# Last two turns of attention: first pair's rows loaded and measured sooner, normalised later, its seven splits reordered between and behind the values

## The chip, the cores and the metric

One Trainium2 chip, one core of it. The metric is the device time of one launch in microseconds. The kernel before is given by the median of three runs. Beside the times there is one profiled execution, from which all rows come.

## What is computed

The reference is one decoder layer over x, 4 sequences of 2048 tokens with 512 features, and a context of 77 tokens per sequence:

```python
x = x + ssm(layernorm(x), ...)                   # a state space layer over the first axis
x = x + xattn(layernorm(x), ctx, Wq, Wk, Wv, Wo) # 16 heads of 32, 77 keys
x = x + mlp(layernorm(x), ...)                   # 512 -> 2048 -> 512, butterflies and gelu between
```

In the kernel the butterflies are folded into two dense weight matrices first, and the MLP works with those.

## The kernel before

All products that matter are made from high and low parts: a float32 tile is copied to a rounded high part by ScalarE (`hi_...`), the low part is the difference, made by VectorE (`lo_...`), and TensorE adds three products (`split3`, L417).

**Attention turns.** The 8192 tokens are 16 groups (NG) of 512, in four tiles (T) of 128. `attn_loop` runs 18 turns, g = 0 to 17. Turn g works on three groups at once: scores and softmax of group g (`has(0)`), the preparation of queries of group g+1 (`has(1)`), values and first projections of group g-1 (`has(-1)`), last projections of group g-2 (`has(-2)`). So turn 15 (NG-1) has scores, values and projections and no queries, turn 16 (NG) has values and projections, turn 17 only projections 2 and 3. Every engine has its own list of the turn's work, written out by hand (`attn_pe`, `attn_act`, `attn_dve`, `norm` on GpSimd), and engines wait for each other by semaphores that count numbered slots. A slot is one bank of PSUM from 4 to 7 (slot number modulo 4) that TensorE fills, ScalarE copies to a high part and VectorE to a low part or adds to a row; TensorE may fill a bank again when VectorE has finished the slot before it there. Scores use banks 0 to 3. An engine never passes over an item of its list.

TensorE's list in turns 15 to 17 is: `turn_p(2,-1)` (transposes of the probabilities of tile 2), `project(2,-2)`, `scores(0)`, `turn_p(3,-1)`, `project(3,-2)`, `scores(1)`, `values(0)` to `values(3)`, `turn_p(0,0)`, `scores(2)`, `project(0,-1)`, `project(1,-1)`, `turn_p(1,0)`, `scores(3)`, less what a turn does not have. The tiles have these names in the profile: es probabilities, pth/ptl/pt the high and low parts of their transposes (p below), aoh/aol those of the values' outputs, x the rows with the attention's result added by `residual`, rmax the maximum in `shift`, rsum and rinv the sums.

**The MLP's first pair.** The MLP works on eight pairs of groups. A pair's rows are loaded to X (`load_x2`, from x2 in DRAM, where `store_x2` has put the results of attention), measured by VectorE (`spread3` for the statistics of four tiles, `moments` for the variance), given the inverse root by GpSimd (`rsqrt`), normalised in place by ScalarE (`apply3`), transposed by TensorE (`turn3`, eight times, into banks 0 to 3 for the first pair), copied to rawx by ScalarE (`raw_x`), and split into seven operands, xth and xtl: B11, T2, B21, T3, T1, T4, B22. Four of them are combinations that VectorE makes in rawx in place (`mix_x`, four of them, each of which overwrites what a split before it has read). For the first pair all this is done in turns 15 to 17, between the attention's own items; for the later pairs it is inside the MLP and is not touched.

The MLP's products for chunk c take the splits in the order B11, T2, B21, T3, T1, T4, B22 (`up`, units A11, S2, A12, S3, S1, A22, S4). The unit waits until `x_split` of its operand have been made.

**Folded weights.** One chunk of the folded weights is prepared in every turn up to 15: loaded to wc_s (`load_wc`), mixed by VectorE (`mix_weights`), rounded by ScalarE to wc_h (`high_weights`), the low part by VectorE (`low_weights`), stored (`store_wc`). SyncE issues all the DMAs, in one list. The MLP's own weights come through a ring of seven buffers, whose first loads wait for the end of `values(3)` in turn 16.

Of the kernel before, what the change touches and what calls it, by code (L numbers as in the profile page):

```python
# [20 lines left out]
def decoder_layer(nc, x, ctxT, log_dt, log_re, lam_im, vt, vinv, wqT, wkT, wvT, woT, wexpT, bexp, upbias,  # L21
# [237 lines left out]
    with ExitStack() as ctx:  # L259
# [77 lines left out]
        SPLIT_ORDER = (B11, T3, T2, B21, B22, T4, T1)  # L337
        MIX_BEFORE = {B11: 0, B21: 0, B22: 0, T3: 1, T2: 2, T4: 3, T1: 4}
# [22 lines left out]
        x_split = lambda p, o: PROD * p + SPLIT_ORDER.index(o) + 1  # L361
# [94 lines left out]
        def _(sp):  # L456
# [162 lines left out]
            load_wc(NG - 1)  # L619
            sp.wait_ge(pe_slot, SLOTS * (NG - 1))  # L620
            load_x2(0)
            load_x2(1)
            store_x2(NG - 1)
# [38 lines left out]
        def _(pool):  # L662
# [83 lines left out]
            def norm(g, has):  # L746
# [8 lines left out]
                for t in range(T):  # L755
                    pool.wait_ge(rinv_ready, T * g + t + 1)
                    e = es[t % 2][:, :, 0:CK].rearrange("p f (h k) -> p f h k", k=L)
                    r = rinv[:, t % 2, :].rearrange("p (f h) -> p f h", f=KC)
                    for f in range(KC):
                        mul = nc.gpsimd.tensor_tensor(e[:, f], e[:, f], r[:, f].unsqueeze(2).broadcast_to([P, HPC, L]), ALU.mult)  # L760
                    mul.then_inc(p_ready, 1)
                    if g == NG - 1 and t == 0:
                        rsqrt(2 * NG, xn2_ready, NG)
                    if g == NG - 1 and t == 2:
                        rsqrt(2 * NG + 1, xn3_ready, 1)
# [43 lines left out]
        def _(act):  # L809
# [114 lines left out]
            def apply3(g):  # L924
                act.wait_ge(ln_ready, 2 * NG + g + 1)
                xs = X[:, g % 2 * T:(g % 2 + 1) * T]
                apply(xs, xs, xn3_ready)
# [8 lines left out]
            def hi_x3(p, o):  # L936
                act.wait_ge(x3_raw, 8 * p + 8)
# [16 lines left out]
            def attn_act(g, has):  # L954
# [39 lines left out]
                if g == NG:  # L994
                    apply3(1)
# [3 lines left out]
                if g == NG:  # L999
                    for i in range(4, 8):  # L1000
                        raw_x(0, i, i - 4, FIRST_TURN[i])
# [3 lines left out]
                if g == NG:  # L1005
                    load_table(ACT.Gelu)
# [3 lines left out]
                    hi_x3(0, T3)  # L1010
                hi_v(0)
                hi_x(0)
                if g == NG:
                    hi_x3(0, T2)
# [3 lines left out]
                if g == NG:  # L1018
                    hi_x3(0, B21)
                hi_v(2)  # L1020
                hi_v(3)
                if 1 <= g < NG:
                    high_weights(g)
                if g == NG - 1:
                    apply3(0)
                if g == NG:
                    for o in SPLIT_ORDER[4:]:
# [5 lines left out]
                hi_p(0, 0)  # L1033
                hi_x(2)
# [77 lines left out]
        def _(dve):  # L1112
# [239 lines left out]
            def split_first(a, b):  # L1352
                for o in SPLIT_ORDER[a:b]:
                    if MIX_BEFORE[o]:
                        mix_x(0, MIX_BEFORE[o] - 1)
                    lo_x3(0, o)

# [7 lines left out]
            def attn_dve(g, has):  # L1365
# [60 lines left out]
                residual(2, -2)  # L1426
                shift(0)
                if g == NG - 1:
                    spread3(0)
                lo_p(3, -1)  # L1430
                sums(0)
                if g == NG - 1:
                    moments(2 * NG)
                residual(3, -2)
                if g == NG:
                    split_first(0, 2)
                    mix_x(0, 1)
                if g == NG + 1:
                    split_first(6, PROD)
# [5 lines left out]
                if g == NG:  # L1445
                    lo_x3(0, T2)
# [3 lines left out]
                if g == NG:  # L1450
                    split_first(3, 4)
                lo_v(2)
                lo_v(3)
                if g == NG:
                    split_first(4, 5)
# [6 lines left out]
                if g == NG - 1:  # L1462
                    spread3(1)
                lo_x(2)
                residual(0, -1)
                sums(2)
                if g == NG - 1:
                    moments(2 * NG + 1)
                lo_x(3)
                residual(1, -1)  # L1470
                if g == NG:
                    split_first(5, 6)
                lo_p(1, 0)
                shift(3)
# [3 lines left out]
                if 0 <= g < NG:  # L1478
                    low_weights(g, 0)
                sums(3)  # L1480
                if 0 <= g < NG:
# [139 lines left out]
        def _(pe):  # L1621
# [146 lines left out]
            def attn_pe(g, has):  # L1768
# [86 lines left out]
                if g == NG:  # L1855
                    for i in range(4):
                        pe.wait_ge(x3_raw, i + 1)
                        turn3(0, FIRST_TURN[4 + i], i)
# [10 lines left out]
                values(3)  # L1869
                turn_p(0, 0)  # L1870
# [163 lines left out]
```

## Time and profile before

| | us |
|---|---|
| three runs, median | 2355.14 |
| three runs, lowest and highest | 2351.54, 2356.56 |
| the profiled execution, its time | 2351.65 |
| its span | 2349.9 |
| TensorE busy in the span | 2219.8 (94%) |
| VectorE, ScalarE, GpSimd busy | 1770.7, 1291.4, 557.8 |

Times in the profile are counted from the span's start. A row of the timeline gives the start, the duration and, in brackets, how long the engine had been idle before it and what it had waited for. "x4" are four instructions in a row, given as one. The granted clock is TensorE's, as a share of full speed.

### The profile page before, as it was taken

Reading aid. Unit: us, or ns where it says so; the run is one execution under the profiler, and the core shown is the slowest. Engines: PE = TensorE matmul, PEld = TensorE weight load, DVE = VectorE, ACT = ScalarE, POOL = GpSimd, SP = SyncE. Lnnn points to the kernel's source line nnn. Section 1 sums busy time; section 2 is a strip of 40 time slices with the busy share of each in tenths; the row PEclk is TensorE's granted clock in tenths of the full one; section 3 lists DMA queues with packets and bytes.
Section 4 is the critical chain, followed back from the end, with each engine's and each line's share of the span. In section 5 each row is a group of like instructions: output and inputs, shape, how many; then the busy total and the mean of one; then the engine's idle time right before and its main releaser. Section 6 shows DMA issues by size and latency. Waiting matters only on the chain.

```text
span 2349.9 us, 42242 instructions
## 1 busy us (share of the span) xinstructions
PE 2219.8 (94%) x15752; PEld 1938.0 (82%) x15752; DVE 1770.7 (75%) x2969; ACT 1291.4 (55%) x2832; POOL 557.8 (24%) x619
## 2 busy tenths in 40 slices
PE   8777889999999999779999999999999999999998
PEld 4777668777778777658998988988989989889898
DVE  5999678888888888655866857947858768578567
ACT  2998556576576676444544635535445446355343
POOL 3788222232222222200030030120300300300203
PEclk9888879999999999999999999999999999999999
DMA  8555712332332332247667676685686686776765
GB/s 332 192 179 183 261 53 78 117 125 77 114 121 84 108 111 77 95 159 231 200 197 251 208 238 207 207 265 172 216 267 184 204 267 199 225 222 207 226 188 178
DMA packets 190883, 424.47 MB, mean 181 GB/s; under 512 B 27342, under 2 KB 64718, under 8 KB 190286
## 3 DMA queue, kind: packets, MB, share of 16 engines
q1 hardware_dynamic: 190696, 421.94, 55.6%
q8 instruction: 121, 1.98, 0.3%
q14 instruction: 66, 0.54, 0.1%
HBM read 331.29 MB, written 90.60 MB: 180 GB/s over the span
## 4 chain that ended last, share of the span: by engine, by line
PE 66%; DVE 17%; ACT 10%; issue 4%; POOL 1%; DMA 1%; DVEq 0%; ACTq 0%; SPq 0%; POOLq 0%
PE ps L417 53%; PE ps L1831 5%; ACT es L986 5%; PE ps L1799 2%; DVE st L1165 2%; DVE gl L1194 2%; DVE G L1556 2%; DVE ptl L1194 2%; PE ps L1810 1%; DVE wc_s L1194 1%; DVE rmax L1406 1%; ACT wc_h L943 1%; DVE rsum L1417 1%; ACT pth L961 1%; DVE pt L1194 1%
## 5 line engine op out<-in xcount | busy, mean ns | idle before, releaser
L417 PE MATMUL ps<-ring,gh 128*128 128x256 f32 x3584 | 654.4, 285 | 12.5 <-DVE gl L1194 12.4
L417 PEld LDWEIGHTS ps<-ring,gh 128*128 128x128 f32 x3584 | 558.0, 192 | 16.7 <-DVE gl L1194 15.7
L417 PE MATMUL ps<-xth,ring 128*128 128x512 f32 x1792 | 553.4, 389 | 1.0 <-ACT U L1082 1.0
L417 PE MATMUL ps<-ring,gl 128*128 128x256 f32 x1792 | 506.7, 283 | 0.0
L417 PEld LDWEIGHTS ps<-xth,ring 128*128 128x128 f32 x1792 | 336.4, 188 | 71.1 <-issue 1.4
L1070 ACT ACTIVATE gh<-G 128x512 fp32r<-128x512 f32 x384 | 236.8, 628 | 212.5 <-PE ps L417 212.2
L417 PE MATMUL ps<-xtl,ring 128*128 128x512 f32 x896 | 348.6, 389 | 0.0
L417 PEld LDWEIGHTS ps<-ring,gl 128*128 128x128 f32 x1792 | 343.4, 192 | 0.0
L1194 DVE TENSOR_TENSOR gl<-G,gh 128x512 fp32r<-128x512 f32 x384 | 278.1, 736 | 57.1 <-ACT gh L1070 55.5
L760 POOL TENSOR_TENSOR es<-es,rinv 128x308 f32<-128x308 f32 x256 | 180.8, 738 | 454.6 <-DVE rinv L1421 454.6
L1496 DVE TENSOR_TENSOR U<-ps,U 128x512 f32<-128x512 f32 (+1 forms) x168 | 137.2, 817 | 168.1 <-PE ps L417 165.4
L1053 ACT ACTIVATE G<-G,up_b 128x512 f32<-128x512 f32 x192 | 138.9, 723 | 222.0 <-DVE G L1496 222.0
L1496 DVE TENSOR_TENSOR G<-ps,U 128x512 f32<-128x512 f32 x192 | 132.8, 692 | 123.5 <-PE ps L417 123.0
L695 POOL TENSOR_TENSOR rstd<-var_e,mhalf 128x4 f32<-128x4 f32 x48 | 55.2, 1150 | 611.6 <-DVE var_e L1183 611.6
L417 PEld LDWEIGHTS ps<-xtl,ring 128*128 128x128 f32 x896 | 168.2, 188 | 34.5
L986 ACT ACTIVATE es<-ps,rmax 128x77 f32<-128x77 f32 x512 | 157.9, 338 | 61.6 <-DVE rmax L1406 61.5
L789 POOL TENSOR_TENSOR X<-X,U 128x256 f32<-128x256 f32 x64 | 72.7, 1167 | 488.3 <-DVE U L1496 488.3
L1053 ACT ACTIVATE G<-ps,up_b 128x512 f32<-128x512 f32 x64 | 44.2, 690 | 135.6 <-PE ps L417 135.6
L1810 PE MATMUL ps<-ident,es 128*128 128x128 f32 (+1 forms) x768 | 104.0, 284 | 15.3 <-DVE xt2l L1194 5.7
L417 PE MATMUL ps<-woh,aoh 128*128 128x512 f32 x256 | 106.9, 417 | 10.5 <-DVE ptl L1194 6.6
L778 POOL TENSOR_TENSOR X<-X,ob 128x512 f32<-128x512 f32 x64 | 86.2, 1379 | 126.8 <-DMA X<-x_scratch 113.1
L961 ACT ACTIVATE pth<-ps 128x512 fp32r<-128x512 f32 x128 | 69.6, 597 | 83.6 <-PE ps L1810 83.6
(212 smaller groups left out, 4638.0 us busy)
## 6 DMA issues: line engine op xcount, KB each, us to landing
ring<-wup_scratch SPq DMA_DIRECT2D x224, 512.0 KB, 3.9
ring<-wdn_scratch SPq DMA_DIRECT2D x224, 512.0 KB, 3.6
X<-x_scratch SPq DMA_DIRECT2D x32, 1024.0 KB, 8.4
xa<-in_x SPq DMA_DIRECT2D x16, 1024.0 KB, 5.3
x_scratch<-xa SPq DMA_DIRECT2D x16, 1024.0 KB, 4.3
x<-x_scratch SPq DMA_DIRECT2D x16, 1024.0 KB, 5.6
x_scratch<-x SPq DMA_DIRECT2D x16, 1024.0 KB, 4.3
out_x<-X SPq DMA_DIRECT2D x16, 1024.0 KB, 6.3
```

Of the source, the lines that this page charges most:

```text
L417: mm = pe.matmul(bank, a, b, start=first and i == 0, stop=last and i == n - 1, skip_group_check=go_on)
L760: mul = nc.gpsimd.tensor_tensor(e[:, f], e[:, f], r[:, f].unsqueeze(2).broadcast_to([P, HPC, L]), ALU.mult)
L778: x = tt(X[:, i * T + t, :], X[:, i * T + t, :], ob[:, :], ALU.add)
L789: ins = tt(x, x, U[:, u + t // 2, t % 2 * HW:(t % 2 + 1) * HW], ALU.add)
L961: his.done(A(out, bank, ACT.Copy), hi_slot(n))
L986: e = A(es[t % 2][:, f, h * L:(h + 1) * L], ps[:, h, f * LP:f * LP + L], ACT.Exp, bias=rmax[:, t % 2, at:at + 1], accum_out=rsum[:, t % 2, ...
L1053: A(dst, dst if src is None else src, ACT.Gelu, bias=up_b[:, chunk:chunk + 1]).then_inc(gelu_done, 1)
L1070: A(gh[e % GR][:, :], src, ACT.Copy).then_inc(g_hi, 1)
L1194: sub = lambda o, a, b: V.tensor_tensor(o, a, b.bitcast(F32), ALU.subtract)
L1496: add = lambda o, a, b: V.tensor_tensor(o, a, b, ALU.add)
L1810: mm = pe.transpose(b[0:keys.shape[1], j * P:(j + 1) * P], keys, ident[:, :])
L1831: mm = pe.matmul(b[0:VW[c]], v[:, f, V_AT[c]:V_AT[c + 1]], pt, start=(i == 0), stop=(i == len(passes) - 1))
```

## The change

On SyncE the two loads of X for the first pair are issued ahead of the last load of folded weights and no longer behind it. On VectorE the first group is still measured in turn 15, but behind the low parts of p, and its moments come after `shift(2)`; the second group is measured in turn 16 and no longer in 15. In turn 15 ScalarE rounds the folded weights behind the high parts of p; VectorE's low weights move ahead of and behind `sums(2)`, and `shift(3)` goes ahead of `lo_p(1,0)`. ScalarE normalises the first group in turn 16, and the second in turn 16 in two halves between the high parts of the values' outputs. TensorE makes the second four transposes behind the values and not ahead of them, and with them go the raw copies, the load of the Gelu table and the splits: only B11 is ahead of the values' outputs, B21 behind them, T3 and T2 in turn 16, T1, T4 and B22 in turn 17. GpSimd's two inverse roots stand one product later. Context is cut here:

```diff
 SPLIT_ORDER = (B11, T3, T2, B21, B22, T4, T1)
+FIRST_ORDER = (B11, B21, T3, T2, T1, T4, B22)
 MIX_BEFORE = {B11: 0, B21: 0, B22: 0, T3: 1, T2: 2, T4: 3, T1: 4}
...
 split = lambda p, e: UNITS * p + e + 1
-x_split = lambda p, o: PROD * p + SPLIT_ORDER.index(o) + 1
+x_split = lambda p, o: PROD * p + (SPLIT_ORDER if p else FIRST_ORDER).index(o) + 1
...
     store_wc(NG - 2)
-    load_wc(NG - 1)
     sp.wait_ge(pe_slot, SLOTS * (NG - 1))
...
     load_x2(1)
+    load_wc(NG - 1)
     store_x2(NG - 1)
...
             mul.then_inc(p_ready, 1)
-            if g == NG - 1 and t == 0:
+            if g == NG - 1 and t == 1:
                 rsqrt(2 * NG, xn2_ready, NG)
-            if g == NG - 1 and t == 2:
+            if g == NG - 1 and t == T - 1:
                 rsqrt(2 * NG + 1, xn3_ready, 1)
...
             apply2(1)
-    def apply3(g):
+    def apply3(g, a=0, b=T):
         act.wait_ge(ln_ready, 2 * NG + g + 1)
         xs = X[:, g % 2 * T:(g % 2 + 1) * T]
-        apply(xs, xs, xn3_ready)
+        for t in range(a, b):
+            ins = apply_tile(xs, xs, t)
+        if b == T:
+            ins.then_inc(xn3_ready, 1)
...
     def hi_x3(p, o):
-        act.wait_ge(x3_raw, 8 * p + 8)
+        act.wait_ge(x3_raw, 8 * p + (8 if p or o not in (B11, B21) else 4))
         after(act, x3_mix, 4 * p + MIX_BEFORE[o])
...
         if g == NG:
-            apply3(1)
+            apply3(0)
             for i in range(4):
...
         hi_p(3, -1)
-        if g == NG:
-            for i in range(4, 8):
-                raw_x(0, i, i - 4, FIRST_TURN[i])
         exp(0)
...
         if g == NG:
-            load_table(ACT.Gelu)
             act.wait_ge(x2_stored, 16 * (NG - 2))
...
             hi_x3(0, B11)
-            hi_x3(0, T3)
         hi_v(0)
...
         if g == NG:
-            hi_x3(0, T2)
+            apply3(1, 0, 2)
         exp(1)
...
         if g == NG:
-            hi_x3(0, B21)
+            apply3(1, 2, T)
         hi_v(2)
         hi_v(3)
-        if 1 <= g < NG:
+        if 1 <= g < NG - 1:
             high_weights(g)
-        if g == NG - 1:
-            apply3(0)
         if g == NG:
-            for o in SPLIT_ORDER[4:]:
+            hi_x3(0, B21)
+            for i in range(4, 8):
+                raw_x(0, i, i - 4, FIRST_TURN[i])
+            load_table(ACT.Gelu)
+            for o in FIRST_ORDER[2:]:
                 hi_x3(0, o)
...
         hi_p(0, 0)
+        if g == NG - 1:
+            high_weights(g)
         hi_x(2)
...
-    def split_first(a, b):
-        for o in SPLIT_ORDER[a:b]:
-            if MIX_BEFORE[o]:
-                mix_x(0, MIX_BEFORE[o] - 1)
-            lo_x3(0, o)
-
     def lo_x3(p, o):
...
         residual(2, -2)
+        if g == NG:
+            spread3(1)
+        if g == NG + 1:
+            mix_x(0, 3)
+            lo_x3(0, T1)
         shift(0)
+        lo_p(3, -1)
         if g == NG - 1:
             spread3(0)
-        lo_p(3, -1)
         sums(0)
-        if g == NG - 1:
-            moments(2 * NG)
+        if g == NG:
+            moments(2 * NG + 1)
         residual(3, -2)
         if g == NG:
-            split_first(0, 2)
-            mix_x(0, 1)
+            lo_x3(0, B11)
         if g == NG + 1:
-            split_first(6, PROD)
+            lo_x3(0, T4)
+            lo_x3(0, B22)
         shift(1)
...
             mix_weights(g)
-        if g == NG:
-            lo_x3(0, T2)
         sums(1)
...
         lo_x(1)
-        if g == NG:
-            split_first(3, 4)
         lo_v(2)
...
         if g == NG:
-            split_first(4, 5)
+            lo_x3(0, B21)
+            mix_x(0, 0)
         if isinstance(g, int) and g == 0:
...
         if g == NG - 1:
-            spread3(1)
+            moments(2 * NG)
         lo_x(2)
         residual(0, -1)
+        if g == NG - 1:
+            low_weights(g, 0)
+        if g == NG:
+            mix_x(0, 1)
+            lo_x3(0, T3)
+            lo_x3(0, T2)
         sums(2)
         if g == NG - 1:
-            moments(2 * NG + 1)
+            low_weights(g, 1)
         lo_x(3)
...
         if g == NG:
-            split_first(5, 6)
+            mix_x(0, 2)
+        if g == NG - 1:
+            shift(3)
         lo_p(1, 0)
-        shift(3)
+        if not (g == NG - 1):
+            shift(3)
         if isinstance(g, int) and g == 0:
...
         lo_q(0)
-        if 0 <= g < NG:
+        if 0 <= g < NG - 1:
             low_weights(g, 0)
         sums(3)
-        if 0 <= g < NG:
+        if 0 <= g < NG - 1:
             low_weights(g, 1)
...
         project(3, -2)
-        if g == NG:
-            for i in range(4):
-                pe.wait_ge(x3_raw, i + 1)
-                turn3(0, FIRST_TURN[4 + i], i)
         start = isinstance(g, int) and g == 0
...
         values(3)
+        if g == NG:
+            for i in range(4):
+                pe.wait_ge(x3_raw, i + 1)
+                turn3(0, FIRST_TURN[4 + i], i)
         turn_p(0, 0)
...
         turn_x(2)
```

## Rows read from the trace of the kernel before

**Rows 1.** windows: busy us (instructions) of each engine, granted clock, DMA share, GB/s
```profile
970.00:974.00 4.00, 3.99 (x10) 2.85 (x11) 3.86 (x11) 0.17 (x1) 2.85 (x5) 0.53 0.02 4
951.00:1007.00 56.00, 41.19 (x362) 32.34 (x360) 40.72 (x73) 29.66 (x97) 13.30 (x21) 0.91 0.28 97
1007.00:1050.00 43.00, 31.50 (x134) 24.29 (x135) 21.46 (x25) 17.16 (x26) 0.63 (x1) 0.88 0.46 170
1050.00:1200.00 150.00, 148.25 (x949) 135.24 (x949) 110.73 (x171) 75.20 (x116) 9.67 (x9) 1.00 0.69 213
```

**Rows 2.** timeline, TensorE: start, us, instruction, idle before, releaser
```profile
963.26 0.32 PE L1799 MATMUL ps<-kh,ql 32*128 32x78 f32 x4
970.01 0.79 PE L1831 MATMUL ps<-pth,vh 128*128 128x512 f32 x1 [6.44 <-DVE pt L1194]
...
1007.68 2.68 PE L1810 MATMUL ps<-ident,es 128*128 128x128 f32 x12 [3.08 <-POOL es L760]
...
1025.22 0.80 PE L1831 MATMUL ps<-pth,vh 128*128 128x512 f32 x1 [6.16 <-DVE aol L1194]
...
1045.66 0.39 PE L417 MATMUL ps<-xth,ring 128*128 128x512 f32 x1
...
1049.53 0.47 PE L417 MATMUL ps<-xth,ring 128*128 128x512 f32 x1 [0.98 <-ACT U L1082]
```

**Rows 3.** timeline, VectorE, turn 15
```profile
965.58 2.47 DVE L1165 BATCH_NORM_STATS2 st<-X 128x6 f32<-128x512 f32 x4 [5.91 <-DMA X<-x_scratch]
...
970.99 0.10 DVE L1177 TENSOR_TENSOR msum<-st 128x4 f32<-128x4 f32 x1
...
973.11 0.67 DVE L1397 TENSOR_TENSOR x<-x,ps 128x512 f32<-128x512 f32 x1
...
986.19 1.29 DVE L1194 TENSOR_TENSOR ptl<-ps,pth 128x512 fp32r<-128x512 f32 x2 [4.19 <-ACT pth L961]
...
999.17 0.80 DVE L1406 TENSOR_REDUCE rmax<-ps 128x8 f32<-128x616 f32 x1
...
1001.43 1.22 DVE L1194 TENSOR_TENSOR wc_s<-wc_s,wc_h 128x1024 f32<-128x1024 f32 x1
```

**Rows 4.** timeline, ScalarE, turns 15 and 16
```profile
981.17 1.69 ACT L943 ACTIVATE wc_h<-wc_s 128x1792 fp32r<-128x1792 f32 x1
982.76 2.92 ACT L817 ACTIVATE X<-X,nmr,rstd 128x512 f32<-128x512 f32 x4
...
1014.09 2.07 ACT L934 ACTIVATE rawx<-ps 128x512 f32<-128x512 f32 x4 [3.10 <-PE ps L1763]
1016.18 1.28 ACT L947 ACT_TABLE_LOAD   x1
...
1017.58 1.04 ACT L939 ACTIVATE xth<-rawx 128x1024 fp32r<-128x1024 f32 x1
```

**Rows 5.** chain that ended last, 951 to 1050: start, us, what
```profile
952.79 3.03 PE ps L417 x12
...
957.84 7.72 DMA X<-x_scratch
...
976.68 3.97 PE ps L1831 x16
...
1019.88 1.15 DVE rawx L1338
...
1025.22 5.41 PE ps L1831 x16
```

**Rows 6.** timeline, GpSimd, the last product of turn 15
```profile
1004.37 3.26 POOL L760 TENSOR_TENSOR es<-es,rinv 128x308 f32<-128x308 f32 x4 [5.85 <-DVE rinv L1421]
```

**Rows 7.** SyncE timeline; DMA issues, 948 to 968, with us to landing
```profile
949.45 0.67 SPq L588 DMA_DIRECT2D wdn_scratch<-wc_s  x1
...
X<-x_scratch SPq DMA_DIRECT2D x2, 1024.0 KB, 8.7
...
wdn_scratch<-wc_s SPq DMA_DIRECT2D x1, 896.0 KB, 7.0
```

## The prediction

> **What bounds the kernel now.** I read the windows first. After attention, in the MLP, TensorE is busy 148.25 of 150 us [rows 1]: nothing outside it is worth anything there. Ahead lie two poor stretches, 951 to 1007 (41.19 of 56 us busy) and 1007 to 1050 (31.50 of 43), with a mean clock of 0.91 and 0.88. They hold 26 us of idle TensorE, and the whole change lies in them: turn 15 begins at 951.2, turn 16 near 1005, turn 17 near 1040. The first MLP product is the row at 1045.66, and from 1049.53 TensorE flows [rows 2]. What counts is how much earlier that point comes; the MLP behind it only repeats itself.
>
> Then the timelines, for who waits for whom. (1) 970.01: `values(0)` of turn 15 waits 6.44 us for VectorE's `pt` [rows 2]. VectorE stood at `spread3(0)`: 5.91 us for X, 2.47 us of measuring, and only then `ptl` [rows 3]. (2) 976.68: `values(2)` [rows 5] comes 1 us after `values(1)` has ended, when `aol` is done, behind sums, moments and shift. (3) `ptl` at 986.19 waited 4.19 us for ScalarE [rows 3], which did `wc_h` (981.17) and four normalisations (982.76) first [rows 4]. (4) 1007.68: TensorE waits 3.08 us for GpSimd's `es`. (5) 1025.22: `values(2)` of turn 16 waits 6.16 us for `aol` [rows 2], since second raw copies (1014.09), table load (1016.18) and two splits with their mixes stand ahead of it on ScalarE and VectorE [rows 4]. (6) Up to 1049.53 three short waits behind mixes and splits.
>
> **The change part by part.** Prices: four normalisations 2.92, four raw copies 2.07, a high split 1.05, `wc_h` 1.6, table load with its dummy 1.4 (1016.18 to 1017.58) [rows 4]; four measurements 2.47, moments 2.1 (970.99 to 973.11), a shift 2.26 (999.17 to 1001.43), a residual 0.6, a low part of 512 columns 0.6 [rows 3]; a low split or a mix 1.15, a projection 3.0, two `values` 3.97 at full clock and 5.41 if they begin after a long wait [rows 5]; GpSimd's four products 2.7 to 3.3 [rows 6].
>
> *Turn 15.* The low parts of p now stand ahead of `spread3(0)`: they start when the shift ends, 959.6 (965.58 less the idle 5.91, rounded down for overlap), and take 2.0 us (three times 0.6 and hops), to 961.6. `values(0)` is then held only by `scores(1)`, to 963.5 (the row at 963.26 and its 0.32) [rows 2]: 6.5 us earlier. X is issued when turn 14's queries end (951.4: the projection at 952.79 [rows 5] less twelve transposes) instead of at 957.84; X(0) took 7.72 us to land [rows 5], which gives 959.2. It is now behind two stores instead of two small loads; the second store, issued 949.45 with 7.0 us, lands at 956.5. The second X lands about 9.7 us from issue (median of the two 8.7) with an issue 0.6 later, so 1 MB takes 2.5 us [rows 7]: behind the stores X(0) lands at 959.0, in shares with them by 963. VectorE asks for it at 961.6. I count no wait; bounds 0 and 4 us (landing at 965.6, as now).
>
> The Trainium skill, DMA: Bandwidth & Descriptors (section Queues, rings and completion order), says that descriptors of one ring are consumed in ring order; by that rule X comes behind the stores, 959, and the sum stays as it is. In the trace X landed behind the smaller loads issued before it, which agrees.
>
> The wc loads (two of 256 KB) still go when the store has landed, at 956.5, but behind 2 MB of X: that ends at 961.5 to 963.7, so they land at 963 to 965. `mix_weights` reaches them at 968.5, so 3 us of cover; past that each us costs one.
>
> VectorE from there: measured 964.0, sums 965.0, residual 965.6, shift 967.9, `aol` 968.5. `values(2)` starts at 968.6, 8.1 earlier (the slow clock is gone), and `values(3)` ends 972.4. ScalarE goes from `aoh` straight to p, as `wc_h` and the normalisation are behind or gone: `ptl` at 973.6 instead of 986.19, 12.6 earlier. VectorE: p 975.5, shift 977.8, moments 979.9, residual 980.5, low weights 981.7, sums 982.7, low weights 983.5, residual 984.1; `shift(3)` at 984.1 instead of 999.17, 15.0 earlier, to 986.4; p 988.3, sums 989.3. `wc_h` (974.3 to 975.9) lies ahead of `exp(2)`, which waits for the shift until 976.3: hidden by 0.4.
>
> *Turn 16, with work added in front.* TensorE needs the banks of `lo_p(1,0)`, now behind `shift(3)`: projection 2 from 988.4, on a clock that has probably fallen (5 us with little work; at 1007.68 twelve transposes took 2.68 after 3.08 us of waiting), 993.0. ScalarE: p 989.4, `apply3(0)` 992.3. TensorE: four turns 994.6, p (GpSimd's product 989.3 to 992.6 is in time) 996.1, projection 3 to 999.0. VectorE: p 991.3, residual 993.5, `spread3(1)` 996.0, p 997.9; so `values(0)` at 999.0. The added 2.9 us on ScalarE and 2.5 on VectorE lie beside GpSimd's product and TensorE's projections. VectorE: moments 1000.1, residual 1000.7, B11 1001.9, `aol` 1002.5, inside `values(0)` and `values(1)`. `values(2)` follows at 1002.9 instead of 1025.22: 22.3 earlier, the largest step. The halves of `apply3(1)` (1.5 us each) lie between `aoh` copies; cover ends if `aol` of slot 8 comes past 1002.9, and the first half stands behind its `aoh`.
>
> *Behind the values.* Values end 1006.8, against 1030.6 (1025.22 and 5.41 [rows 5]). Four turns 1008.5, projections 0 to 2 until 1016.8. ScalarE: B21 1008.4, raw copies 1010.4, table 1011.8, T3 1012.9. VectorE paces: mix 1011.5, residual 1012.1, mix 1013.3, T3 1014.4, T2 1015.6, residual 1016.2, mix 1017.3, residual 1017.9. Projection 3 runs 1018.0 to 1020.9, and there the MLP begins: 14.1 us behind the values, where now it is 15.1. T1 is split at 1021.5 and S1 needs it at 1026.3; T4 and B22 (1024.4) come before their products too. Table load: the row's 1.4 us, hidden behind residual and mix by 0.4.
>
> The Trainium skill, ScalarE: Activation LUTs (section What ACT_TABLE_LOAD costs), adds a drain of 1.38 us to 1.28 us of load; by it T3, and the MLP's start, come 1.0 us later. The trace has the next split 1.4 us behind the load's start, so I take the row.
>
> First product at 1020.9 instead of 1045.66, 24.8 earlier; and the 0.98 us wait for U at 1049.53 goes, as ScalarE's splits end at 1022.3. **Sum: 6.5 (X, p ahead) + 1.6 (clock) + 4.5 (`wc_h`, normalisation) + 2.4 (measuring and moments from before `shift(3)`) + 8.8 (turn 16, to the values' end) + 1.0 (tail) + 1.0 (U) = 25.8 us.** The profiled execution took 2351.65 us around its span of 2349.9, and is at the low end of the three runs; against it I would say 2325.9, against the median, 2355.14, it is 2329.
>
> **Rivals.** (A) As above, 2329; its own range is 2325 to 2334: 4 us for X, 1 for hops. (B) New waits take half: X late (4), wc late (3), `lo_p(1,0)` behind `shift(3)` (2 to 3), B11's split or `apply3` ahead of `values(2)` (2 to 3): 12 us lost, 2341. For it speaks that some places have only 0.4 us of cover; against it that no single one costs over 4. (C) TensorE's clock stays low. Over 970 to 974 it was granted 0.53 [rows 1], mostly the lower of its two levels (1.2 GHz), after the 6.44 us wait. Two `values` cost 1.44 us more there, a projection about as much; for four pairs and eight projections 17 us, of which some 10 would lie on the path: 2339. Against it: my timetable has one pause over 3 us (983.7 to 988.4) where there are five. The Trainium skill, TensorE: Matmul & The Clock Gate (section Loop structure matters more than you think), hangs the clock on the pauses between matmuls, which speaks the same way. (D) No change: the time is given back at the MLP, because its first weights are late. Their loads wait for `values(3)` before and after, and the distance to use only falls from 15.1 to 14.1 us, with no wait for a load in that start now: 2355 would take 25 us of it. (E) Slower, by the wc loads behind X. `aol` and all of p stand behind `mix_weights` on VectorE, one us for each us late. It decides from a landing at 968.5+25.8 = 994.3, 38 us from issue; at 1000 it is 2361. X with 1 MB needed 7.72.
>
> **How the numbers follow.** A 0.72, B 0.12, C 0.09, D 0.04, E 0.03. Likeliest 2329. A measurement tells 0.2%, 4.7 us, from no change; A, B and C lie beyond it: faster 0.93, same 0.04, slower 0.03. Range 2322 (the runs' half spread of 2.5, and 4 if the clock holds at 988 and hops overlap) to 2341 (C and the near end of B).
>
> **What would show it.** Right: `values(0)` of turn 15 near 963.6 at full clock; no DMA wait at `spread3(0)`; `ptl` near 973.6; `values(2)` of turn 16 right behind `values(1)`; the first product with xth near 1021 and no pause for U. Wrong: a DMA wait on `st` or `wc_s`; a granted clock under 0.9 over 990 to 1020. The prediction falls if the first product comes later than 1036, or if from there to the end it takes longer than now, 2349.9 less 1045.66.

## The result, and the profile after

The changed kernel takes 2324.22 us (median of four runs, 2324.05 to 2326.55), the kernel before 2353.59 (four runs, 2351.54 to 2356.56). The ratio is 0.9884, 95% interval 0.9872 to 0.9896: 1.16% faster, 27.3 us of 2353.59; the two medians themselves lie 29.4 us apart. The span of the profiled execution fell from 2349.9 to 2322.2, by 27.7 us. Of the ten executions of the kernel before beside experiments 5 to 8 two took 2496 and 12281 us, which moves their median by 0.5 us. Lines are numbered otherwise in the changed kernel than in the one before: `turn_p` L1818 for L1810, `values` L1839 for L1831, `lo_...` L1197 for L1194, the residual L1394 for L1397, `shift` L1403 for L1406.

The windows come first, with the columns of [rows 1]:

```profile
970.00:974.00 4.00, 4.00 (x53) 3.26 (x51) 3.22 (x7) 2.63 (x6) 2.67 (x4) 1.00 0.01 2
951.00:1007.00 56.00, 51.94 (x434) 42.02 (x433) 45.70 (x84) 38.04 (x112) 14.37 (x20) 0.97 0.43 146
1007.00:1050.00 43.00, 41.60 (x184) 34.10 (x183) 26.51 (x33) 18.63 (x27) 1.29 (x1) 1.00 0.70 241
1050.00:1200.00 150.00, 148.25 (x986) 136.87 (x985) 111.28 (x168) 72.59 (x112) 22.91 (x20) 1.00 0.68 208
```

The two poor stretches are now busy 51.94 of 56 and 41.60 of 43 us, with clocks of 0.97 and 1.00. They held 26.3 us of idle TensorE before and hold 5.5 now. Over the same work, from the first product of `scores(1)` in turn 15 to the first MLP product, TensorE was busy 58.89 of 83.62 us at a mean clock of 0.88 before (962.04 to 1045.66), and 52.77 of 57.61 at 0.97 now (961.52 to 1019.13). So of the 26.0 us won there 19.9 are waits and 6.1 are products that no longer run at the lower clock. In the MLP TensorE is busy 148.25 of 150 us as before.

TensorE's timeline shows where the waits went (columns as in [rows 2]):

```profile
962.99 0.50 PE L1839 MATMUL ps<-pth,vh 128*128 128x512 f32 x1
...
967.99 0.50 PE L1839 MATMUL ps<-pth,vh 128*128 128x512 f32 x1 [1.05 <-DVE aol L1197]
...
984.59 0.66 PE L1818 MATMUL ps<-ident,es 128*128 128x128 f32 x4 [1.44 <-POOL es L761]
986.18 1.79 PE L1818 MATMUL ps<-ident,es 128*128 128x128 f32 x8 [0.94 <-DVE ptl L1197]
987.62 0.78 PE L418 MATMUL ps<-woh,aoh 128*128 128x512 f32 x1
988.20 0.63 PE L418 MATMUL ps<-wol,aoh 128*128 128x512 f32 x1
...
991.59 1.94 PE L1771 MATMUL ps<-ident,X 128*128 128x128 f32 x16
...
997.41 0.39 PE L1839 MATMUL ps<-pth,vh 128*128 128x512 f32 x1
...
1001.08 0.40 PE L1839 MATMUL ps<-pth,vh 128*128 128x512 f32 x1
...
1016.26 0.50 PE L418 MATMUL ps<-woh,aoh 128*128 128x512 f32 x1 [1.40 <-DVE x L1394]
...
1019.13 0.39 PE L418 MATMUL ps<-xth,ring 128*128 128x512 f32 x1
```

The waits of 6.44, 3.61, 3.08 and 6.16 us of [rows 2] (the 3.61 is at 987.02 there, behind `ptl`) are gone. What is left are 1.05, 1.44, 0.94 and 1.40 us (and 0.52 ahead of `scores(1)`, 0.51 before). `values(2)` of turn 16 (1001.08) follows `values(1)` with no wait, and no wait for U stands behind 1019.13. One projection still runs partly at the lower clock: its products take 0.63 us at 988.20, and 0.39 at the full one.

VectorE (columns as in [rows 3]) asks for X without a wait (961.10), reaches the last folded weights without one (967.86), and has `ptl` of tile 0 at 973.21. The moments, seven small instructions from 977.49, end at 978.38: 0.9 us.

```profile
961.10 2.47 DVE L1168 BATCH_NORM_STATS2 st<-X 128x6 f32<-128x512 f32 x4
...
967.86 1.67 DVE L1327 TENSOR_TENSOR wc_s<-wc_s 128x256 f32<-128x256 f32 x4
...
973.21 1.28 DVE L1197 TENSOR_TENSOR ptl<-ps,pth 128x512 fp32r<-128x512 f32 x2
...
977.49 0.15 DVE L1180 TENSOR_TENSOR msum<-st 128x4 f32<-128x4 f32 x1
...
978.38 0.69 DVE L1394 TENSOR_TENSOR x<-x,ps 128x512 f32<-128x512 f32 x1
...
983.20 0.80 DVE L1403 TENSOR_REDUCE rmax<-ps 128x8 f32<-128x616 f32 x1 [0.60 <-PE ps L1807]
```

ScalarE's timeline of turns 15 and 16 shows `wc_h` hidden ahead of `exp(2)`, the normalisation in turn 16, and the table load with the next split 1.4 us after its start:

```profile
973.90 1.70 ACT L947 ACTIVATE wc_h<-wc_s 128x1792 fp32r<-128x1792 f32 x1
976.07 0.33 ACT L990 ACTIVATE es<-ps,rmax 128x77 f32<-128x77 f32 x1 [0.47 <-DVE rmax L1403]
...
988.50 2.94 ACT L818 ACTIVATE X<-X,nmr,rstd 128x512 f32<-128x512 f32 x4
...
1008.49 1.28 ACT L951 ACT_TABLE_LOAD   x1
...
1009.89 1.05 ACT L943 ACTIVATE xth<-rawx 128x1024 fp32r<-128x1024 f32 x1
```

The loads: SyncE's timeline, and then the DMA issues of 948 to 968 with the median us to landing.

```profile
950.92 1.76 SPq L607 DMA_DIRECT2D X<-x_scratch  x2
956.41 1.25 SPq L580 DMA_DIRECT2D wc_s<-wd_scratch  x2
```

```profile
X<-x_scratch SPq DMA_DIRECT2D x2, 1024.0 KB, 10.5
...
wc_s<-wd_scratch SPq DMA_DIRECT2D x2, 256.0 KB, 6.8
```

Both are medians of two loads. Taken one by one, the two of folded weights, issued at 956.41 and 957.03, took 6.3 and 7.3 us, so the second landed at 964.3; both were needed at 967.86. The first group of X took 9.3 us from 950.92 and landed at 960.2, 0.9 us before VectorE asked for it at 961.10. The second took 11.6 and was measured only at 992.30.

### The profile page after: what moved, and what is told of

Read it like the earlier page. It is cut to its first block, busy times and chain, and to the rows that moved or that the text cites. A ratio compares the mean times of both kernels' runs of the same rounds, so it can differ in the third digit from the quotient of the medians.

```text
span 2322.2 us, 42242 instructions
## 1 busy us (share of the span) xinstructions
PE 2213.2 (95%) x15752; PEld 1933.7 (83%) x15752; DVE 1768.1 (76%) x2969; ACT 1291.2 (56%) x2832; POOL 557.8 (24%) x619
## 4 chain that ended last, share of the span: by engine, by line
PE 66%; DVE 17%; ACT 9%; issue 4%; DMA 2%; DVEq 1%; POOL 0%; SPq 0%; ACTq 0%; POOLq 0%
PE ps L418 53%; PE ps L1839 5%; ACT es L990 5%; PE ps L1807 2%; DVE st L1168 2%; DVE gl L1197 2%; DVE G L1564 2%; DVE ptl L1197 2%; PE ps L1818 1%; DMA xa<-in_x 1%; DVE wc_s L1197 1%; DVE rmax L1403 1%; ACT wc_h L947 1%; ACT pth L965 1%; DMA x_scratch<-xa 1%
## 5 line engine op out<-in xcount | busy, mean ns | idle before, releaser
L1197 DVE TENSOR_TENSOR gl<-G,gh 128x512 fp32r<-128x512 f32 x384 | 278.3, 737 | 57.2 <-ACT gh L1073 55.5
L1818 PE MATMUL ps<-ident,es 128*128 128x128 f32 (+1 forms) x768 | 103.4, 283 | 14.4 <-DVE xt2l L1197 5.7
L990 ACT ACTIVATION_READ_ACCUMULATOR es<-ps,rmax 128x1 f32 x512 | 112.2, 219 | 0.0
```

Of the source, the lines that this page charges most:

```text
L990: e = A(es[t % 2][:, f, h * L:(h + 1) * L], ps[:, h, f * LP:f * LP + L], ACT.Exp, bias=rmax[:, t % 2, at:at + 1], accum_out=rsum[:, t % 2, ...
L1197: sub = lambda o, a, b: V.tensor_tensor(o, a, b.bitcast(F32), ALU.subtract)
L1818: mm = pe.transpose(b[0:keys.shape[1], j * P:(j + 1) * P], keys, ident[:, :])
```

## The experiments

The kernels are compared by their medians, and, since differences of two or three us matter, by one distance in the profile as well: from the first product of `scores(1)` in turn 15 (962.04 before, 961.52 after) to the first product with xth (1045.66 and 1019.13). It leaves out what scatters ahead of turn 15. It is read from one execution of each kernel; the changed kernel, profiled twice, gave 57.61 and 57.64, but in 4, 8, 9 and 10 the profiled execution is the slowest of its kernel, 0.5 to 1.6 us above the median. All kernels of one group ran beside the kernel before on the same chip (its medians: 2353.62 beside 1 to 4, 2351.67 beside 5 to 8, and 2353.5 beside the rest).

| kernel | median us | ratio, 95% | distance us |
|---|---|---|---|
| before | 2353.59 | 1 | 83.62 |
| after | 2324.22 | 0.9884 [0.9872, 0.9896] | 57.61 |
| 1 loads and p, in before | 2349.64 | 0.9984 [0.9973, 0.9996] | 80.95 |
| 2 after, wc loads first | 2330.62 | 0.9908 [0.9891, 0.9924] | 63.50 |
| 3 turn 15 alone | 2348.96 | 0.998 [0.997, 0.999] | 80.80 |
| 4 after, `wc_h` ahead | 2325.76 | 0.9883 [0.9866, 0.9899] | 60.07 |
| 5 after, `shift(3)` behind | 2328.09 | 0.9897 [0.9877, 0.9916] | 60.64 |
| 6 after, moments behind `sums(2)` | 2324.06 | 0.9881 [0.9861, 0.99] | 57.84 |
| 7 after, table early | 2325.43 | 0.9887 [0.9868, 0.9907] | 57.66 |
| 8 after, second half ahead | 2344.72 | 0.9971 [0.9958, 0.9983] | 77.05 |
| after, run again | 2324.44 | 0.9876 [0.9859, 0.9892] | 57.64 |
| 9 filled | 2322.42 | 0.9867 [0.985, 0.9883] | 55.49 |
| 10 after, moments behind `sums(1)` | 2326.11 | 0.9883 [0.9866, 0.9899] | 60.38 |
| 11 after, first part undone | 2330.27 | 0.9902 [0.9885, 0.9918] | 64.37 |

The theory: the gain is the sum of the waits removed and of the lower clock behind them, as predicted. The rival: one part makes nearly all of it, and the others only ride on it.

**1. The loads' order and p ahead of the measuring, in the kernel before.**

```diff
-load_wc(NG - 1)
 load_x2(0); load_x2(1)
+load_wc(NG - 1)
...
+lo_p(3, -1)
 if g == NG - 1: spread3(0)
-lo_p(3, -1)
```

> The kernel before with only two edits: X is loaded ahead of the last folded weights, and spread3(0) stands behind the low parts of p. Theory (the chain passes through them and nothing else takes their place): values(0) of turn 15 starts near 963.6, the moments stay ahead of shift(1), so values(2) starts near 970.7 instead of 976.68 and everything behind comes 6 us earlier: 2347 to 2348 against a median of 2353.6. Rival (ScalarE, which ends the wait at 986, takes the gain up): p at 986.19 moves by less than 2 us and the time stays over 2351.

It gave 2.7 us of distance and 4.0 of median. Neither expectation held: the time is above the 2347 to 2348 of the theory, and `ptl` moved by more than the 2 us of the rival. TensorE's timeline says why it is less than the 6.5 by which `values(0)` came sooner (963.70 here):

```profile
970.88 0.80 PE L1831 MATMUL ps<-pth,vh 128*128 128x512 f32 x1 [3.23 <-DVE aol L1194]
971.47 0.63 PE L1831 MATMUL ps<-pth,vl 128*128 128x512 f32 x1
...
982.56 0.77 PE L417 MATMUL ps<-woh,aoh 128*128 128x512 f32 x1 [3.61 <-DVE ptl L1194]
...
1038.79 0.79 PE L417 MATMUL ps<-woh,aoh 128*128 128x512 f32 x1 [2.27 <-DVE x L1397]
1039.38 0.63 PE L417 MATMUL ps<-wol,aoh 128*128 128x512 f32 x1
```

The wait went to `values(2)`, where `aol` still stands behind measuring, sums, 2.1 us of moments and shift, and behind it `values(2)` and `values(3)` took 5.1 us to the next transposes (976.02) instead of 3.8, since they began at the lower clock. `ptl` came 4.5 us sooner (981.73 for 986.19), and that was carried through most of turn 16. At the last projection part of it was lost: behind the same wait of 2.27 us for the same row, its first product takes 0.79 us here and the following 0.63, while before they took 0.50 and 0.40 (1042.77, 1043.11).

**2. The changed kernel with the loads as before.** The edit puts `load_wc(NG - 1)` ahead of the two `load_x2` again.

> The changed kernel with one edit undone: the last folded weights are loaded ahead of X again. Theory (X is asked for at 961.1 and would land near 965.1, as in the kernel before): VectorE waits some 4 us at spread3(0), behind p, so values(0) still starts near 963 but values(2) of turn 15 comes 4 us later, and the end 3 to 4 us: 2327 to 2328. Rival (the place behind p alone removes the wait, the order of the loads is idle): under 1 us, 2324 to 2325.

VectorE then waits for X, in just the size that the prediction kept as its bound:

```profile
964.12 2.47 DVE L1168 BATCH_NORM_STATS2 st<-X 128x6 f32<-128x512 f32 x4 [4.00 <-DMA X<-x_scratch]
```

The distance grew by 5.9, more than the 4.0: `values(2)` waits 5.01 us for `aol` (971.01) and begins at the lower clock, 0.80 and 0.63 us a product; from there to the next transposes are 5.6 us (976.59), in the changed kernel 3.8 (967.99 to 971.78). So 4.0 are the wait and 1.8 the clock. Expected was the wait alone, 2327 to 2328, and measured 2330.62.

**3. Turn 15 alone.** Experiment 1, and with it `high_weights` behind `hi_p(0, 0)`, the low weights around `sums(2)` and `shift(3)` ahead of `lo_p(1, 0)`; the normalisations stay in turn 15 and ahead of the values of turn 16, the second half of the pair too.

> The first kernel of this call plus what else the change does to turn 15 without postponing the normalisation: wc_h behind p on ScalarE, the low weights around sums(2), shift(3) ahead of lo_p(1,0). Measuring, moments and normalisation of both groups stay where they were, and turns 16 and 17 are those of the kernel before. Theory (most of the gain is the normalisation's place and turn 16): another 1.6 us for wc_h, 7 to 9 us in all, 2345 to 2347. Rival (turn 15's order is the greater half): 13 us or more, 2340.

A miss: 2.8 us, hardly more than experiment 1. `wc_h` is out of the way of `ptl`, but what that frees is lost just ahead: behind 3.22 us of wait `values(2)` and `values(3)` take 6.6 us (970.28 to the transposes at 976.91), most of it at the lower clock, where they took 5.1 in experiment 1. `ptl` comes at 981.03, and counted from `scores(1)` that is only 0.1 sooner than in experiment 1. Nothing in which the two kernels differ stands ahead of these products, so the edit did not cause the longer stretch. In turn 16 new waits of 2.85 (994.81, for a residual) and 1.67 us (997.56, for `ptl`) stand where GpSimd's was. The work between these and the last values is untouched.

**4. `wc_h` ahead of p again in turn 15**, in the changed kernel:

```diff
-if 1 <= g < NG - 1:
+if 1 <= g < NG:
     high_weights(g)
...
 hi_p(0, 0)
-if g == NG - 1:
-    high_weights(g)
```

> The changed kernel with wc_h ahead of the high parts of p in turn 15 again. Theory (the 1.6 us lie on the path between values(3) and p): ptl 1.5 us later than its 973.21, of which shift(3)'s own wait for scores(3) absorbs 0.6, so the first MLP product comes near 1020 instead of 1019.1 and the time is 2325 to 2326. Rival (TensorE has the projections to do meanwhile): no change of the first product, 2324.2.

2325.76, 1.5 above the changed kernel, as expected, though the runs of the two overlap; by the distance 2.5, where 0.9 was expected. `ptl` comes 1.5 us later (974.73), as `wc_h` is long. The rest is a fall of the clock inside a projection, behind a wait of only 0.80 us:

```profile
975.57 0.47 PE L418 MATMUL ps<-woh,aoh 128*128 128x512 f32 x1 [0.80 <-DVE ptl L1195]
...
976.10 0.44 PE L418 MATMUL ps<-woh,aol 128*128 128x512 f32 x1
976.35 0.63 PE L418 MATMUL ps<-woh,aoh 128*128 128x512 f32 x1
```

The lower clock lasts until 979.7. From the start of this projection to the transposes behind it and the next are 7.1 us (982.71) instead of 5.6 (974.64 to 980.20), so `scores(3)` come later, and `shift(3)` waits 1.24 us for them at 985.71 where it waited 0.60.

**5. `shift(3)` behind `lo_p(1, 0)` again**, in the changed kernel.

> The changed kernel with shift(3) of turn 15 behind lo_p(1,0) again. Theory (the chain exp(3), the high parts of p, apply3(0) sets when the first transposes of X start, so shift(3) must come first): shift(3) starts at 984.5 instead of 983.2, the transposes and the first product come 1.2 us later, 2325 to 2326. Rival (the banks of lo_p(1,0) are what TensorE waits for at 986.2 and at the slow projection behind it): they come free 3 us sooner and the first product up to 1.4 us earlier, 2323.

```profile
988.00 0.48 PE L418 MATMUL ps<-woh,aoh 128*128 128x512 f32 x1
...
995.05 3.48 PE L1768 MATMUL ps<-ident,X 128*128 128x128 f32 x16 [4.07 <-ACT X L818]
```

2328.09, where 2325 to 2326 were expected. The bank for projection 2 comes sooner and the projection runs at full clock. But `exp(3)`, p and the normalisation behind it on ScalarE come later; the transposes of X wait 4.07 us for it and then take 3.48 instead of 1.94 us. The distance grows by 3.0 instead of 1.2. The prediction's new wait for `lo_p(1,0)` is real (rival B), but the other order costs more.

**6 and 7. Two places that should be hidden.** Six puts the moments of the first group behind `sums(2)`, to bring them beside GpSimd's product; seven puts the table load ahead of B11 in turn 16.

> The changed kernel with the first group's moments of turn 15 one place later, behind sums(2), where GpSimd begins its four products at once. Theory (VectorE's small operations on SBUF are held up by a GpSimd product that runs beside them): the seven operations take 2.1 us, as in the kernel before, and not 0.9, and GpSimd's product is no shorter; the end comes 0.3 to 0.8 us later. Rival (their length in the kernel before had to do with what stood before them on VectorE): 0.9 us, no change.

> The changed kernel with the load of the Gelu table ahead of the split of B11 again, so ahead of the values' outputs. Theory (1.4 us on ScalarE are covered in either place: B11's high part was made 1.8 us before VectorE took it, and in the tail VectorE paces): first product at 1019.1 as before, 2324.2. Rival (the table load was what held aol and the values up in the kernel before): values(2) of turn 16 and all behind it 1 us or more later, 2325.5.

Both leave the time as it is (distances +0.2 and +0.05). Six doesn't decide what it was made for: GpSimd's inverse root stands in its list ahead of that product and waits for the moments, so the product began at 983.54, when they were over, and they took 0.9 us again. In seven the load began at 996.32 and the next split at 997.72, again 1.4 us: the load is covered in either place.

**8. The second half ahead of the values again**: the second four transposes, their raw copies, table load, T3, T2, B21 and the mixes at the places they had before, and the whole second normalisation ahead of the values, behind `hi_p(3, -1)`. Turn 15 stays as changed, and so do the second group's measuring and moments, which stay in turn 16.

> The changed kernel with everything that stands behind the values put back ahead of and between them: the whole of apply3(1), the second four transposes, the raw copies, the table load, the old order of the seven splits. Turn 15 and the first group's postponed normalisation stay as changed. Theory (this is the greater half of the gain): values(0) of turn 16 at 1004 instead of 997.4, since the second normalisation now stands ahead of it, values(2) at 1014 and on a slow clock, first product near 1034, 2338 to 2341. Rival (turn 15 has most of the gain): under 8 us, 2332 or less.

```profile
1003.93 3.65 PE L1773 MATMUL ps<-ident,X 128*128 128x128 f32 x16 [4.85 <-ACT X L818]
...
1017.27 0.79 PE L1841 MATMUL ps<-pth,vh 128*128 128x512 f32 x1 [5.54 <-DVE aol L1199]
...
1035.64 0.68 PE L418 MATMUL ps<-woh,aoh 128*128 128x512 f32 x1 [2.27 <-DVE x L1396]
...
1043.96 0.47 PE L418 MATMUL ps<-xth,ring 128*128 128x512 f32 x1 [0.96 <-ACT U L1087]
```

19.4 us of distance are lost, and the wait for U is back. Expected were 2338 to 2341, measured 2344.72: a miss by 4. But the 19.4 are not all the price of the place ahead of the values. The wait of 4.85 us stands in neither of the two kernels compared: the normalisation at 1000.86 has waited 3.61 us for GpSimd's inverse root, because the moments come only at 998.39, while in the kernel before the second group was measured in turn 15 and its transposes (1013.46) began without a wait. With the slow transposes behind it this is 6.6 us. An estimate for the place alone, 19.4 less 6.6, is 12.8 us, half of the whole. The first three rows each begin a stretch at the lower clock (1.94 us for the first at the full one, 0.50 for the others).

**9. The changed kernel, filled.** By the chain of the changed kernel, TensorE waited at 984.59 and 986.18 and then ran projection 2 slowly. Here the low parts of p go ahead of `shift(3)`, the second part of the low weights behind it, the normalisation of the first group is split over the gaps of ScalarE, and a mix moves from turn 16 to turn 17:

```diff
+if g == NG - 1: apply3(0, 0, 1)   # the first two places: ScalarE
 hi_p(1, 0)
+if g == NG - 1: apply3(0, 1, 3)
 exp(3)
...
 hi_p(2, -1)
-if g == NG: apply3(0)
+if g == NG: apply3(0, 3, T)
...
+if g == NG + 1: mix_x(0, 2)      # from here on: VectorE
...
-if g == NG - 1: low_weights(g, 1)
 lo_x(3)
 residual(1, -1)
-if g == NG: mix_x(0, 2)
-if g == NG - 1: shift(3)
 lo_p(1, 0)
-if not (g == NG - 1): shift(3)
+shift(3)
+if g == NG - 1: low_weights(g, 1)
```

> The changed kernel itself once more, on the chip of the three runs beside it: 2324 with the first product 57.6 us behind the scores(1) of turn 15, as in its first trace.

> The changed kernel with the pauses that its trace still shows filled: in turn 15 lo_p(1,0) stands ahead of shift(3) and the second part of the low weights behind it, three of the first group's four normalisations stand around hi_p(1,0) on ScalarE, where it waits 1.65 and 1.57 us, and only the fourth stays ahead of the transposes; in turn 17 mix_x(0,2) stands behind residual(2,-2). Theory: TensorE's projection 2 of turn 16 runs at 986 on the full clock, the transposes of X start at 989.9 instead of 991.6, projection 3 of turn 17 waits 0.8 us less, and the first product comes 2.2 us earlier: 2322. Rival (the freed places open a pause of over 3 us elsewhere and TensorE's clock falls, as in the runs with one edit undone): no gain or up to 2 us lost, 2324 to 2326.

2322.42 (2321.67 to 2322.88) against 2324.44 (2323.38 to 2325.16) for the changed kernel beside it: 2.0 us, small, but the runs don't overlap, and the distance fell by 2.15. Projection 2 runs at full clock, and the mean clock over the distance is 1.00. The last projection waits 0.85 us for 1.40, so 0.55 less and not 0.8, and a wait of 0.31 for U is new:

```profile
986.17 0.48 PE L418 MATMUL ps<-woh,aoh 128*128 128x512 f32 x1
...
1015.00 0.50 PE L418 MATMUL ps<-woh,aoh 128*128 128x512 f32 x1 [0.85 <-DVE x L1398]
...
1021.07 0.47 PE L418 MATMUL ps<-xth,ring 128*128 128x512 f32 x1 [0.31 <-ACT U L1089]
```

**10. The moments beside GpSimd's product**: directly behind `sums(1)`, to do what six missed.

> The changed kernel with the first group's moments of turn 15 directly behind sums(1), where GpSimd is not held by the inverse root and begins its four products at once. Theory (VectorE's small operations are held up by a GpSimd product that runs beside them): the seven operations take 2.1 us, as in the kernel before, and not 0.9; p of tile 0 comes 1.3 us later, the first product 0.4 to 1 us. Rival (their length has to do with what stood before them): 0.9 us, p where it was, first product where it was.

VectorE's timeline, and then GpSimd's (its four instructions apart):

```profile
971.37 0.10 DVE L1180 TENSOR_TENSOR msum<-st 128x4 f32<-128x4 f32 x1
...
971.65 0.61 DVE L1183 TENSOR_SCALAR nmean<-msum 128x4 f32<-128x4 f32 x1
972.17 0.15 DVE L1184 TENSOR_TENSOR nsq<-nsq 128x4 f32<-128x4 f32 x1
972.36 0.56 DVE L1185 SCALAR_TENSOR_TENSOR sq<-nsq,sq 128x4 f32<-128x4 f32 x1
972.95 0.63 DVE L1186 TENSOR_SCALAR var_e<-sq 128x4 f32<-128x4 f32 x1
973.49 1.87 DVE L1197 TENSOR_TENSOR aol<-ps,aoh 128x512 fp32r<-128x512 f32 x3
```

```profile
971.53 0.70 POOL L761 TENSOR_TENSOR es<-es,rinv 128x308 f32<-128x308 f32 x1 [3.49 <-DVE rinv L1418]
972.19 0.70 POOL L761 TENSOR_TENSOR es<-es,rinv 128x308 f32<-128x308 f32 x1
972.86 0.70 POOL L761 TENSOR_TENSOR es<-es,rinv 128x308 f32<-128x308 f32 x1
973.51 0.70 POOL L761 TENSOR_TENSOR es<-es,rinv 128x308 f32<-128x308 f32 x1
```

The moments take 2.1 us again (971.37 to 973.49), as in [rows 3], against 0.9 in the changed kernel. The distance grew by 2.8 and the median by 1.7 over the changed kernel beside it, both more than the 0.4 to 1 expected, since they also stand ahead of `aol` here: counted from `scores(1)`, projection 2 begins 2.0 us later than in the changed kernel (990.39), and it takes 4.7 us instead of 4.0, as it is longer at the lower clock (0.78 and 0.63 us).

**11. The first part undone inside the changed kernel**: both edits of experiment 1 taken back.

> The changed kernel without its first part: the last folded weights are loaded ahead of X, and spread3(0) stands ahead of the low parts of p. Theory (the first wait is worth in the changed kernel what the sum gave it, 6.5 us and 1.6 us of slow clock): values(0) of turn 15 at 969.5 on a slow clock, first product 7 to 9 us later, 2331 to 2333. Rival (it is worth what it brought when it was added alone, 2.7 us): 2327.

6.8 us of distance, just under the 7 to 9 expected: `values(0)` waits 6.21 us for `pt` (969.29) and begins at the lower clock. The same part gave 2.7 alone (experiment 1), so the parts don't add up. Experiment 2 had lost 5.9 of these 6.8 with only the loads' order taken back: once X is late, p's place is worth 0.9.

## Why the prediction was right

It was 2329.0 with a range of 2322 to 2341; the time is 2324.2, the case is A, and the gain by the profile is 27.7 for 25.8. Its terms against the changed trace, whose times are taken 0.52 us later, since `shift(0)` of turn 15 begins at 956.82 after and at 957.34 before (each row is what is gained up to there beyond the row above):

| term, up to | forecast | measured |
|---|---|---|
| X and p ahead, `values(0)` | 6.5 | 6.5 |
| clock, `values(2)` | 1.6 | 1.7 |
| `wc_h` and normalisation, `ptl` | 4.5 | 4.3 |
| measuring and moments, `shift(3)` | 2.4 | 3.0 |
| turn 16, end of the values | 8.8 | 9.7 |
| tail, first product | 1.0 | 0.8 |
| U, to the end of the span | 1.0 | 1.2 |
| ahead of turn 15 | 0 | 0.5 |
| sum | 25.8 | 27.7 |

- **X and the wc loads.** X was there when VectorE asked, at 961.1 for a forecast of 961.6, but it had landed only at 960.2 and not at 959.0; the folded weights landed at 964.3, in the forecast 963 to 965. The bound of 4 us for X was not drawn. Its size was right: experiment 2 shows it as 4.00. Rival E, folded weights behind X, fell with the landing at 964.3; 3.5 us of cover stood where I counted 3.
- **`wc_h` and the first normalisation** came out as one sum, 4.3 for 4.5. Experiment 4 undoes `wc_h` alone; no experiment puts this normalisation, or the measuring of the second group, back by itself.
- **The moments** were the wrong size. I priced them at the 2.1 us of [rows 3]. In that row GpSimd's product ran beside them (971.15, 2.67 us); at their new places it doesn't, and they take 0.9, twice. In turn 15 that put VectorE 1.2 us ahead, of which TensorE gave back 0.6 (the wait at 983.20). Experiment 10 moved them beside a product again, and they took 2.1.
- **Turn 16.** From `shift(3)` to projection 2 I had 4.3 us, measured 4.4. That the clock would fall there was right; the price was too high: the projection takes 4.0 us to the start of the four transposes (987.62 to 991.59), where I counted 4.6. The `values` were 7.5 instead of 7.8, and from the transposes to `values(0)` 5.8 instead of 6.0.
- **The tail** went as forecast, VectorE pacing with mixes and residuals: 14.2 us for 14.1 from the values' end. The table load cost the 1.4 us of the row and was hidden; experiment 7 shows it covered in turn 16 too.
- **Rival B** (new waits take half) was a matter of size: three such waits are there, 1.44, 0.94 and 1.40 us, with a slow projection behind the first two, and all but the last stand in the forecast's pause ahead of 988.4. **Rival C** (the clock stays low): 0.97 and 1.00 against it, and 1.00 over 990 to 1020, where under 0.9 was named as a sign of being wrong. What is left is some 1.0 us of projection 2 and 0.5 of the eight transposes ahead of it (1.44 us from 986.18 to the projection, where twelve take 1.40 at 971.78). I held against this rival that there are five pauses over 3 us now and one in my timetable. That was a miscount: TensorE's rows before have four, 6.44, 3.61, 3.08 and 6.16. The changed kernel has none over 3 us, and its clock still fell at 986, behind 1.44 and 0.94, in the pause that the forecast had at 983.7 to 988.4. The mechanism itself shows in the experiments: in 1 to 5, 8, 10 and 11 such a stretch, new or longer, lies in the distance. **Rival D** (given back in the MLP): the part behind the first product took 1303.07 us against 1304.24, so nothing came back.

So the mechanism was right, term by term within 1 us, and no large error cancels another. What is left are the 4.8 us between 2329.0 and 2324.2: 1.9 are the terms above. The other 2.9 come from the base: I took the 25.8 off the first median, 2355.14, which lay 3.5 us over the profiled execution; from the profiled execution it would have been 2325.9, and the changed kernel's own median lies within 0.2 us of its profiled execution (2324.07).

The rival of the experiments, that one part does it, is half right. The second half behind the values is the largest part, an estimated 12.8 us of 26.0 (experiment 8), but on a changed turn 15; what had been changed there in experiment 3 gave 2.8 with the second half in its old place. A part is worth what the waits behind it leave of it. What the second half would bring by itself, in the kernel before, no experiment shows.

## What to carry to other kernels

Price a reordering by a timetable from engine to engine, up to the point from which the bounding engine flows, and add to each wait what the lower clock costs behind it: here 1.4 to 1.8 us for transposes or two `values` (3.48 and 3.65 for 1.94 in experiments 5 and 8, 5.41 for 3.97 in [rows 5], 5.6 for 3.8 in experiment 2) and 1.0 for projection 2. Don't judge a part by trying it alone: the same two edits were worth 2.7 us alone and 6.8 as the last to be made. And take over a small instruction's duration, or a median, only with what stands beside it: the engines busy in its row, and the median's distance to the profiled execution.

## What the runs showed of the hardware

**VectorE's small instructions beside GpSimd's product.** In experiment 10, `nmean`, `sq` and `var_e` take 0.61, 0.56 and 0.63 us where they take 0.17, 0.16 and 0.17 with GpSimd idle. They end at 972.26, 972.92 and 973.58, within 0.1 us behind the starts of GpSimd's next instructions (972.19, 972.86, 973.51), and `nsq`, which begins at such a boundary (972.17), takes 0.15. That fits waiting for the running instruction of GpSimd to end, and not a slower run. `msum` and `sq<-st` had begun here before the product did at 971.53; in experiment 3, where the second group's moments (991.23) fall inside a product (990.58, 3.26 us), they take 0.65 and 0.67 as well. In experiment 10 GpSimd loses nothing, 2.68 us for its four. In the changed kernel the product at 981.27 took 3.26 us, beside VectorE's low weights (981.11, 0.90), whose operands all lie in SBUF. The Trainium skill, SBUF — State Buffer (section SBUF: two separate sides), says that VectorE and GpSimd share a pair of ports under an exclusive lock, held for a whole instruction, for VectorE's instructions with two inputs from SBUF and those in its two-port mode; the rows agree for `sq`, and `nmean` and `var_e`, with one tensor as input, would have to be in that mode, which no row shows.

**The clock hangs on more than the last wait.** Behind a wait of 2.27 us for the same residual, the last projection ran at full clock in the kernel before (0.50 and 0.40 us a product at 1042.77) and at the lower one in experiments 1, 3 and 8 (0.79 at 1038.79, 0.80 at 1038.11, 0.68 at 1035.64, then 0.63). In experiment 4 the clock fell 0.8 us after a wait of 0.80 us, in the middle of a projection. And experiments 1 and 3, whose work is the same up to 976, ran 7 and 14 products of `values(2)` and `values(3)` below full clock, behind waits of 3.23 and 3.22 us. So a part of this is not fixed by the kernel; what decides it is not settled by the runs, and a distance read from one execution can be off by some 1.5 us where such a stretch lies in it. What a fall costs is read above from durations of the same work at either level. What experiments 4 and 10 would have lost without it is an estimate only, as no experiment holds the clock and changes the delay: in experiment 10 the slower projection is 0.8 of the 2.8 us; in experiment 4 VectorE was ready for `shift(3)` 1.2 us late, and the wait for `scores(3)` makes up the rest of the 2.5.
